# A decoder layer on one core: where cross-attention's inverse row sums are spread, and how many products the routing logits take

## The chip, the cores and the metric

One core of a Trainium2 chip runs one program. The metric is device time in microseconds, the median over runs. The engines are TensorE (PE; its weight loads, PEld, overlap the products), VectorE (DVE), ScalarE (ACT), GpSimd (POOL) and SyncE (SP), which issues the transfers.

## What is computed

A decoder layer on 16 sequences of 128 tokens, width 512, fp32: self-attention, cross-attention with a context, and a mixture of experts with routing. Only cross-attention and the routing logits are touched:

```python
probs = jax.nn.softmax(scores, axis=-1)            # 16 heads, clipped and masked scores
probs = probs / (probs.sum(axis=-1, keepdims=True) + 1e-08)
ctx = jnp.einsum('bhst,bhtd->bhsd', probs, v)      # heads of 32 columns
delta = ctx @ Wo.T + bo                            # then scaled, normed, added to x
...
logits = x @ gate_weight.T                         # x normed again, 64 experts
scores = jax.nn.softmax(logits, axis=-1)
```

## The kernel before

Three phases follow each other, each ended by a barrier: `self_phase`, `cross_phase` (324 to 647 us of the trace) and `feed_forward`. Every fp32 product that needs its precision is split in a high and a low half and done as three products (`matmul3`, L41 to L43: low by high, high by low, high by high).

`cross_phase` walks over the 16 sequences t, which this text calls steps; a step is taken to run from one `scores` to the next. The order on each engine is written out by hand in the loops over t, and semaphores tie the engines together. TensorE does in step t: `scores(t)` (L1967); `widen(t - 1)` (L1994); a projection ("unit") of 12 products for a later sequence; in even steps from 4 on `positions` (L2056 to L2061), which waits until the first half of step t's scores has been read, and from 6 on later `table_part` (L2082), which waits for the second half; a second unit; `turn_final(t - 2)` (transposes of the normed result); `project_out(t - 1)`; `logits(t - 2)`; a third unit; `sums(t)` (L1976) and `attend_v(t)` (L1987). Steps 0 to 11 have three units each; steps 12 and 13 have none, steps 14 and 15 two each, of the shared expert. In steps 3, 7 and 11 all units are queries, and the second needs the bank that ACT empties of the third unit of the step before only after `exps(t, 0)`.

The softmax is normed after the product with the values. `sums(t)` leaves the 16 row sums of a sequence in one bank: row 32 j + c holds head 4 c + j. VectorE inverts all 128 rows (`row_sums`, L1682). The `widen` of the next step multiplies the inverses by four 0/1 matrices (`spread`), which fills a bank with each inverse repeated over its head's 32 rows, ACT copies it to SBUF (`rinv_out`, L1470), and VectorE multiplies the attended values by it (`attn_out`, L1688).

VectorE does in step t: `delta(t - 2)` (L1709 to L1717); `bounded(t, 0)` (L1674, half of the scores); `attn_out(t - 1)`; `bounded(t, 1)`; `attn_lo(t - 1)` (from step 12 on on POOL); in even steps from 4 on `place_tokens` and `keep_slots` (L1793 to L1831); `x_lo` (L1667); in odd steps from 3 on `rank_experts` (L1735 to L1754); `final_lo(t - 2)` (L1722, from step 12 on on POOL), which frees TensorE's logits; statistics; `output(t - 1)` (L1701 to L1705) after the output projection; `route_max(t - 2)` (L1727), the greatest logit, read from PSUM; in odd steps from 3 on `choose_experts` (L1762 to L1783); `row_sums(t)`. ACT's `route_exp` (L1550) reads the logits from PSUM too and frees their bank. After step 15 the same pieces run out in a tail, in which VectorE ranks and places the last two groups of tokens and completes the table of the experts' tokens that the next phase starts from (L1910).

Of the kernel before, what the change touches and what calls it, by code (L numbers as in the profile page):

```python
# [6 lines left out]
F32R = mybir.dt.float32r  # L7
# [953 lines left out]
def cross_uses():  # L961
# [3 lines left out]
    for t in range(BATCH + 2):  # L965
        units = cross_units(t)
        proj += units[0:2]
        ex[1] += [("rb", t - 1)] if 1 <= t <= BATCH else []
# [13 lines left out]
def cross_phase(nc, x_in, ctx_in, pieces, vecs, out_x, stage, kept, early, route, ident, shared):  # L982

    with ExitStack() as ctx:
# [25 lines left out]
        gate = [sb("gate_hi", [P, KC, E], F32R), sb("gate_lo", [P, KC, E], F32R)]  # L1010
# [17 lines left out]
        spread = sb("spread", [P, KC, HPC, HD])  # L1028
# [51 lines left out]

        lneg = sb("lneg", [P, BATCH])
# [41 lines left out]
        s_sum, s_rinv, s_rb = sem("sums_in_psum"), sem("rinv_ready"), sem("rinv_in_psum")  # L1123
# [7 lines left out]
        s_lg, s_lm = sem("logits_in_psum"), sem("logit_max_ready")  # L1131
# [136 lines left out]
        def _(pool):  # L1268
# [66 lines left out]
            def constants():  # L1335
# [4 lines left out]
                lk(pool.memset(spread[:], 0.0))  # L1340
                lk(pool.affine_select(out=spread[:], in_=spread[:], pattern=[[-1, KC], [-HD, HPC], [0, HD]],
                                      compare_op=ALU.not_equal, fill=1.0, base=0, channel_multiplier=1))
# [62 lines left out]
        def _(act):  # L1405
# [60 lines left out]
            def rinv_out(t):  # L1466
                act.wait_ge(s_rb, t + 1)
                if t:
                    act.wait_ge(s_er[0], exchanged(0, ("pv", t - 1)))
                act.activation(rb[:], ex[1][:], ACT.Copy).then_inc(s_er[1], 1)  # L1470

# [73 lines left out]
            def route_exp(t):  # L1545
                g = group_of(t)
                act.wait_ge(s_lm, t + 1)
                if g >= 2:
                    act.wait_ge(s_choice, g - 1)
                act.activation(prob[g % 2][:, t - CROSS_GROUPS[g][0], :], ex[0][:, 0:E], ACT.Exp, bias=lneg[:, t:t + 1],  # L1550
                               accum_out=lsum[:, t:t + 1]).then_inc(s_er[0], 1)
# [7 lines left out]
            for t in range(BATCH):  # L1559
# [6 lines left out]
                if t >= 1:  # L1566
                    rinv_out(t - 1)
# [37 lines left out]
            rinv_out(BATCH - 1)  # L1605
# [22 lines left out]
        def _(dve):  # L1628
# [49 lines left out]
            def row_sums(t):  # L1678
                dve.wait_ge(s_sum, t + 1)
                if t:  # L1680
                    dve.wait_ge(s_rb, t)
                dve.reciprocal(rinv[:], ex[1][:, 0:P]).then_inc(s_er[1], 1)  # L1682

            def attn_out(t):
                dve.wait_ge(s_pv, t + 1)
                dve.wait_ge(s_er[1], exchanged(1, ("rb", t)))
# [38 lines left out]
            def route_max(t):  # L1725
                dve.wait_ge(s_lg, t + 1)
                dve.tensor_reduce(lneg[:, t:t + 1], ex[0][:, 0:E], AX, ALU.max, negate=True).then_inc(s_lm, 1)  # L1727

            def rank_experts(g):
# [4 lines left out]
                dve.wait_ge(s_er[0], exchanged(0, ("lg", b - 1)))  # L1734
# [109 lines left out]
            for t in range(BATCH):  # L1844
# [5 lines left out]
                if t >= 1:  # L1850
                    attn_out(t - 1)
# [36 lines left out]
            one, two, three = range(NG - 3, NG)  # L1888
            delta(BATCH - 2)
# [23 lines left out]
        def _(pe):  # L1913
# [77 lines left out]
            def widen(t):  # L1991
                out = exchange(1, ("rb", t))
                for c in range(KC):
                    ins = pe.matmul(out[:, c * P:(c + 1) * P], spread[:, c, :, :].rearrange("p j d -> p (j d)"), rinv[:],  # L1994
                                    start=True, stop=True)
                ins.then_inc(s_rb, 1)

# [12 lines left out]
            def logits(t):  # L2010
                out = exchange(0, ("lg", t))[:, 0:E]
# [5 lines left out]
                for k in range(KC):  # L2017
                    ins = matmul3(pe, out, (hi[:, k, :], lo[:, k, :]), (gate[0][:, k, :], gate[1][:, k, :]),
                                  k == 0, k == KC - 1)
                ins.then_inc(s_lg, 1)  # L2020

            def shared_unit(i):
# [6 lines left out]
                else:  # L2029
# [3 lines left out]
                    elif i == EARLY + 1:  # L2033
                        pe.wait_ge(s_er[1], exchanged(1, ("rb", BATCH - 1)))
# [51 lines left out]
            for t in range(BATCH):  # L2086
# [3 lines left out]
                if t >= 1:  # L2090
                    widen(t - 1)
# [37 lines left out]
            widen(BATCH - 1)  # L2129
# [1040 lines left out]
```

## Time and profile before

| | |
|---|---|
| three runs | 1549.15, 1557.19, 1557.39 us; median 1557.19 |
| profiled execution, first to last instruction | 1550.6 us |
| its busy time | PE 1471.4 (95%), DVE 1132.1 (73%), ACT 959.0 (62%), POOL 724.0 (47%) |
| cross-attention in it | from 324 to 647 us |

The profiled execution shows no time of its own beside its span, 1550.6 us, which lies between the fastest run and the median. Busy shares are averages over three very different phases; what matters is the stretch from 324 to 647 us and who waits there for whom.

### The profile page before, as it was taken

The numbers are of one execution on the slowest core, as the hardware profiler recorded it, in microseconds if no ns is written. First come the engines' busy times: TensorE is split into PE (matmuls) and PEld (weight loads), VectorE is DVE, ScalarE is ACT, GpSimd is POOL, SyncE is SP. The second block draws the span as 40 slices with busy tenths as digits, with TensorE's granted clock in tenths as the row PEclk, the third lists the DMA queues.
The fourth block names the chain that finished last, engine by engine and source line by source line (L and its number), as shares of the span: only waits on it lengthen the run. The fifth ranks groups of instructions, "written<-read, shape, count | busy, mean of one in ns | idle before, by whom it ended". The sixth has DMA issues, their size and how long they took to land.

```text
span 1550.6 us, 30285 instructions
## 1 busy us (share of the span) xinstructions
PE 1471.4 (95%) x10344; PEld 1217.4 (79%) x10344; DVE 1132.1 (73%) x2021; ACT 959.0 (62%) x1897; POOL 724.0 (47%) x894
## 2 busy tenths in 40 slices
PE   6999998999999979599999999999999999999898
PEld 4788887778888767488888888888888888776675
DVE  6677666745888788777777787777777787757666
ACT  4566566644566566677777777777777777731111
POOL 2122225242232155356565655556565655447573
PEclk9999999999999999899999999999999999999999
DMA  6012112332221231398787778777787778567574
GB/s 211 1 63 82 51 60 70 103 93 75 63 76 42 71 108 38 122 370 298 265 296 265 262 259 286 271 268 262 265 297 265 261 261 285 183 213 246 149 216 156
DMA packets 116629, 280.25 MB, mean 181 GB/s; under 512 B 17984, under 2 KB 23104, under 8 KB 116544
## 3 DMA queue, kind: packets, MB, share of 16 engines
q1 hardware_dynamic: 98800, 228.25, 43.4%
q0 software_dynamic: 15360, 50.34, 10.1%
q8 instruction: 52, 0.85, 0.2%
q10 hardware_dynamic: 2384, 0.53, 0.2%
q14 instruction: 33, 0.27, 0.1%
HBM read 235.69 MB, written 43.38 MB: 180 GB/s over the span
## 4 chain that ended last, share of the span: by engine, by line
PE 48%; DVE 3%; issue 2%; POOL 2%; DMA 1%; another core or an unknown queue 1%; ACT 0%; DVEq 0%; SPq 0%; POOLq 0%
PE e_gu L2608 19%; PE e_gu L2610 9%; PE e_dn_rest L2636 6%; PE e_tr L49 3%; PE e_dn_main L41 3%; PE e_dn_main L43 3%; PE e_dn_main L42 3%; DVE h_acc L2901 2%; POOL h_yk L2818 1%; DMA h_yk<-y_dram,h_idx 1%; DVE h_h_raw L2932 0%; DMA e_raw_u<-in_L_ffn_Wu_dram 0%; DVE h_hid L2917 0%; PE h_gt L41 0%
## 5 line engine op out<-in xcount | busy, mean ns | idle before, releaser
L2371 POOL TENSOR_TENSOR e_hid<-e_h_raw,e_hid 128x128 fp32r<-128x128 f32 (+1 forms) x192 | 165.6, 863 | 223.4 <-ACT e_hid L2436 223.4
L2608 PE MATMUL e_gu<-e_xT_hi_lo,e_wg 128*128 128x384 f32 (+1 forms) x768 | 231.9, 358 | 0.6 <-issue 0.6
L2608 PE MATMUL e_gu<-e_xT_hi_lo,e_wu 128*128 128x384 f32 (+1 forms) x768 | 230.6, 356 | 0.0
L2610 PE MATMUL e_gu<-e_xT_hi_lo,e_wu 128*128 128x192 f32 (+1 forms) x768 | 193.4, 252 | 0.0
L2610 PE MATMUL e_gu<-e_xT_hi_lo,e_wg 128*128 128x192 f32 (+1 forms) x768 | 193.2, 252 | 0.0
L2379 POOL TENSOR_TENSOR e_wd<-e_raw_d,e_wd 96x512 fp32r<-96x512 f32 x64 | 131.4, 2053 | 36.1 <-ACT e_wd L2421 36.1
L2431 ACT ACTIVATE e_low<-e_gu 128x384 f32<-128x384 f32 (+1 forms) x192 | 93.2, 486 | 83.5 <-PE e_gu L2610 56.2
L2514 DVE TENSOR_TENSOR e_total<-e_gu,e_low 128x384 f32<-128x384 f32 (+1 forms) x192 | 105.6, 550 | 53.3 <-issue 44.5
L2608 PEld LDWEIGHTS e_gu<-e_xT_hi_lo,e_wg 128*128 128x128 f32 (+1 forms) x768 | 138.3, 180 | 5.8 <-issue 1.6
L2610 PEld LDWEIGHTS e_gu<-e_xT_hi_lo,e_wg 128*128 128x128 f32 (+1 forms) x768 | 140.1, 182 | 1.4
L2608 PEld LDWEIGHTS e_gu<-e_xT_hi_lo,e_wu 128*128 128x128 f32 (+1 forms) x768 | 137.9, 180 | 3.8
L2610 PEld LDWEIGHTS e_gu<-e_xT_hi_lo,e_wu 128*128 128x128 f32 (+1 forms) x768 | 139.8, 182 | 0.0
L2503 DVE TENSOR_TENSOR e_wg<-e_raw_g,e_wg 128x1408 fp32r<-128x1408 f32 x64 | 104.0, 1625 | 45.6 <-ACT e_wg L2412 45.6
L2818 POOL DMA_INDIRECT h_yk<-y_dram,h_idx x96 | 103.3, 1076 | 28.7 <-issue 25.5
L2421 ACT ACTIVATE e_wd<-e_raw_d 128x1024 fp32r<-128x1024 f32 (+1 forms) x128 | 106.4, 831 | 0.0
L2520 DVE TENSOR_TENSOR e_h_raw<-e_total,e_h_raw 128x192 f32<-128x192 f32 (+1 forms) x192 | 84.7, 441 | 27.8 <-ACT e_h_raw L2426 27.8
L2503 DVE TENSOR_TENSOR e_wu<-e_raw_u,e_wu 128x1408 fp32r<-128x1408 f32 x64 | 103.9, 1623 | 1.1 <-ACT e_wu L2412 1.1
L2359 POOL DMA_INDIRECT e_xg<-xf_dram,e_idx x93 | 93.0, 1000 | 22.1 <-issue 16.7
L2412 ACT ACTIVATE e_wg<-e_raw_g 128x1408 fp32r<-128x1408 f32 x64 | 88.3, 1380 | 10.2 <-DMA e_raw_g<-in_L_ffn_Wg_dram 10.2
L505 ACT ACTIVATE s_prb<-s_prb,s_nmax 128x128 f32<-128x128 f32 x256 | 80.0, 393 | 23.2 <-DVE s_nmax L632 23.1
L2636 PE MATMUL e_dn_rest<-e_raw_d,e_h_raw 128*64 128x512 f32 (+1 forms) x384 | 89.5, 601 | 0.0
L2412 ACT ACTIVATE e_wu<-e_raw_u 128x1408 fp32r<-128x1408 f32 x64 | 88.0, 1375 | 1.0 <-DMA e_raw_u<-in_L_ffn_Wu_dram 1.0
(426 smaller groups left out, 3953.7 us busy)
## 6 DMA issues: line engine op xcount, KB each, us to landing
e_raw_g<-in_L_ffn_Wg_dram SPq DMA_DIRECT2D x64, 704.0 KB
e_raw_u<-in_L_ffn_Wu_dram SPq DMA_DIRECT2D x64, 704.0 KB
e_raw_d<-in_L_ffn_Wd_dram SPq DMA_DIRECT2D x64, 512.0 KB, 6.2
y_dram<-e_y_main SPq DMA_DIRECT2D x64, 256.0 KB
e_raw_d<-in_L_ffn_Wd_dram SPq DMA_DIRECT2D x64, 192.0 KB, 7.5
y_dram<-e_y_rest SPq DMA_DIRECT2D x64, 128.0 KB
s_xr<-in_x_dram SPq DMA_DIRECT2D x16, 256.0 KB, 4.1
x_dram<-s_x SPq DMA_DIRECT2D x16, 256.0 KB, 2.7
```

The lines of the kernel that those rows point to most:

```text
L2359: pool.indirect_dma_start(out=xg[:, j * H:(j + 1) * H], out_offset=None, in_=xf, in_offset=bass.IndirectOffsetOnAxis(ap=ids[:, j:j + 1], a ...
L2371: pool.tensor_tensor(hid[b][1][0:n, c, :], h_raw[g.odd][b][0:n, c, 0:P], hid[b][0][0:n, c, :].bitcast(F32), ALU.subtract).then_inc(s_hl, 1)
L2379: pool.tensor_tensor(wd[b][1][0:96, 2, :], raw_d[g.odd][b][0:96, 2, :], wd[b][0][0:96, 2, :].bitcast(F32), ALU.subtract).then_inc(s_dp[b], 1)
L2412: act.activation(w[b][0][:], raw[b][:], ACT.Copy).then_inc(s_guh[b], 1)
L2421: act.activation(wd[b][0][0:rows, cs, :], raw_d[g.odd][b][0:rows, cs, :], ACT.Copy).then_inc(s_dh[b], 1)
L2431: act.activation(low[m][0:n], gu[m][0:n, :, CAP:2 * CAP], ACT.Copy).then_inc(s_low, 1)
L2503: dve.tensor_tensor(w[b][1][:], raw[b][:], w[b][0][:].bitcast(F32), ALU.subtract).then_inc(s_gul[b], 1)
L2514: dve.tensor_tensor(total[0:n, c], gu[m][0:n, :, 0:CAP], low[m][0:n], ALU.add).then_inc(s_sum, 1)
L2608: pe.matmul(bank[0:n, 0:2 * CAP], w[b][0][:, k, m:m + n], xT[:, :, k, toks], start=k == 0, stop=False)
L2610: ins = pe.matmul(bank[0:n, 0:CAP], w[b][1][:, k, m:m + n], xT[:, 0, k, toks], start=False, stop=k == KC - 1)
L2636: ins = pe.matmul(dn_rest[b * REST:(b + 1) * REST, :], h_raw[g.odd][b][0:n, c, P:CAP], raw_d[g.odd][b][0:n, c, :], start=c == 0, stop=c == 2)
L2818: pool.indirect_dma_start(out=yk[b][:, k * H:(k + 1) * H], out_offset=None, in_=y_in, in_offset=bass.IndirectOffsetOnAxis(ap=idx[b][:, k:k ...
```

## The change

`widen`, `rinv_out` and the constant `spread` go. In their place VectorE does `spread_rinv(t - 1)`, four shuffles of 128 rows by 128 columns from `rinv` to `rb`, each within groups of 32 rows, between `bounded(t, 0)` and `attn_out(t - 1)`; in the tail right after the last `row_sums`, ahead of `delta(14)`. The two halves of the gate's weights lie side by side, so that the high half of x is multiplied by both in one product of 128 columns, and the low half by the gate's high half in one of 64: 8 products instead of 12. The logits then stand in two halves in PSUM; VectorE adds them into an SBUF tile (`tensor_reduce` over the pair), waits for that, and takes the maximum; `route_exp` reads the SBUF tile. The exchange bank of the logits is freed by the addition, not by ACT.

```diff
@@ -965,7 +965,6 @@
         proj += units[0:2]
-        ex[1] += [("rb", t - 1)] if 1 <= t <= BATCH else []
         ex[1] += [("x", m) for m in cross_fresh(t)]
@@ -1007,7 +1006,8 @@
         wo = [sb("wo_hi", [P, KC, H], F32R), sb("wo_lo", [P, KC, H], F32R)]
-        gate = [sb("gate_hi", [P, KC, E], F32R), sb("gate_lo", [P, KC, E], F32R)]
+        gate_both = sb("gate_hi_lo", [P, KC, 2, E], F32R)
+        gate = [gate_both[:, :, half, :] for half in range(2)]
         bias_q = kept["bias_q"]
@@ -1025,7 +1025,6 @@
         pick = sb("pick", [P, KC, HD])
-        spread = sb("spread", [P, KC, HPC, HD])
         iota8 = sb("iota8", [P, GROUPS])
@@ -1078,6 +1077,7 @@
 
+        logit = sb("logit", [P, E])
         lneg = sb("lneg", [P, BATCH])
@@ -1120,7 +1120,7 @@
         s_sc, s_exp, s_clip = sem("scores_in_psum"), sem("exp_ready"), sem("scores_bounded")
-        s_sum, s_rinv, s_rb = sem("sums_in_psum"), sem("rinv_ready"), sem("rinv_in_psum")
+        s_sum, s_rb = sem("sums_in_psum"), sem("rinv_spread")
         s_pv, s_ah, s_al = sem("pv_in_psum"), sem("attnT_hi_ready"), sem("attnT_lo_ready")
@@ -1128,7 +1128,8 @@
         s_ft, s_fh, s_fl = sem("xfT_in_psum"), sem("xfT_hi_ready"), sem("xfT_lo_ready")
-        s_lg, s_lm = sem("logits_in_psum"), sem("logit_max_ready")
+        s_lg, s_lm = sem("logit_halves_in_psum"), sem("logit_max_ready")
+        s_le = sem("logit_exp_ready")
         s_choice, s_pos, s_posr = sem("choice_ready"), sem("positions_in_psum"), sem("positions_read")
@@ -1337,9 +1338,6 @@
                 lk(pool.memset(pick[:, 0, KC:HD], 1.0))
-                lk(pool.memset(spread[:], 0.0))
-                lk(pool.affine_select(out=spread[:], in_=spread[:], pattern=[[-1, KC], [-HD, HPC], [0, HD]],
-                                      compare_op=ALU.not_equal, fill=1.0, base=0, channel_multiplier=1))
                 pool.memset(mark[:], 0.0).then_inc(s_pick, 1)
@@ -1463,12 +1461,6 @@
 
-            def rinv_out(t):
-                act.wait_ge(s_rb, t + 1)
-                if t:
-                    act.wait_ge(s_er[0], exchanged(0, ("pv", t - 1)))
-                act.activation(rb[:], ex[1][:], ACT.Copy).then_inc(s_er[1], 1)
-
             def attn_hi(t):
@@ -1547,8 +1539,8 @@
                     act.wait_ge(s_choice, g - 1)
-                act.activation(prob[g % 2][:, t - CROSS_GROUPS[g][0], :], ex[0][:, 0:E], ACT.Exp, bias=lneg[:, t:t + 1],
-                               accum_out=lsum[:, t:t + 1]).then_inc(s_er[0], 1)
+                act.activation(prob[g % 2][:, t - CROSS_GROUPS[g][0], :], logit[:], ACT.Exp, bias=lneg[:, t:t + 1],
+                               accum_out=lsum[:, t:t + 1]).then_inc(s_le, 1)
 
@@ -1563,8 +1555,6 @@
                         split_hi(n)
-                if t >= 1:
-                    rinv_out(t - 1)
                 exps(t, 0)
@@ -1602,7 +1592,6 @@
                     shared_hi(i)
-            rinv_out(BATCH - 1)
             shared_out(4)
@@ -1678,12 +1667,20 @@
                 if t:
-                    dve.wait_ge(s_rb, t)
+                    dve.wait_ge(s_rb, KC * t)
                 dve.reciprocal(rinv[:], ex[1][:, 0:P]).then_inc(s_er[1], 1)
+
+            def spread_rinv(t):
+
+                dve.wait_ge(s_er[1], exchanged(1, ("sum", t)))
+                if t:
+                    dve.wait_ge(s_er[0], exchanged(0, ("pv", t - 1)))
+                for c in range(KC):
+                    dve.stream_shuffle(rb[:, c * P:(c + 1) * P], rinv[:], [c] * HD).then_inc(s_rb, 1)
 
...
                 dve.wait_ge(s_pv, t + 1)
-                dve.wait_ge(s_er[1], exchanged(1, ("rb", t)))
+                dve.wait_ge(s_rb, KC * (t + 1))
                 dve.wait_ge(s_al, t + 1)
@@ -1724,14 +1721,19 @@
                 dve.wait_ge(s_lg, t + 1)
-                dve.tensor_reduce(lneg[:, t:t + 1], ex[0][:, 0:E], AX, ALU.max, negate=True).then_inc(s_lm, 1)
+                if t:
+                    dve.wait_ge(s_le, t)
+                dve.tensor_reduce(logit[:], ex[0][:, 0:2 * E].rearrange("p (h e) -> p e h", h=2), AX, ALU.add
+                                  ).then_inc(s_er[0], 1)
+                dve.wait_ge(s_er[0], exchanged(0, ("lg", t)))
+                dve.tensor_reduce(lneg[:, t:t + 1], logit[:], AX, ALU.max, negate=True).then_inc(s_lm, 1)
 
...
                 grouped = pr.rearrange("p t (g n) -> p (t g) n", g=GROUPS)
-                dve.wait_ge(s_er[0], exchanged(0, ("lg", b - 1)))
+                dve.wait_ge(s_le, b)
                 link(dve.reciprocal(lsum[:, a:b], lsum[:, a:b]))
@@ -1848,6 +1850,7 @@
                 if t >= 1:
+                    spread_rinv(t - 1)
                     attn_out(t - 1)
@@ -1886,6 +1889,7 @@
             one, two, three = range(NG - 3, NG)
+            spread_rinv(BATCH - 1)
             delta(BATCH - 2)
@@ -1988,13 +1992,6 @@
 
-            def widen(t):
-                out = exchange(1, ("rb", t))
-                for c in range(KC):
-                    ins = pe.matmul(out[:, c * P:(c + 1) * P], spread[:, c, :, :].rearrange("p j d -> p (j d)"), rinv[:],
-                                    start=True, stop=True)
-                ins.then_inc(s_rb, 1)
-
             def project_out(t):
@@ -2008,15 +2005,16 @@
             def logits(t):
-                out = exchange(0, ("lg", t))[:, 0:E]
+                out = exchange(0, ("lg", t))
                 if t < LAST - 2:
...
                 for k in range(KC):
-                    ins = matmul3(pe, out, (hi[:, k, :], lo[:, k, :]), (gate[0][:, k, :], gate[1][:, k, :]),
-                                  k == 0, k == KC - 1)
+                    pe.matmul(out[:, 0:2 * E], hi[:, k, :], gate_both[:, k, :, :].rearrange("p h e -> p (h e)"),
+                              start=k == 0, stop=False)
+                    ins = pe.matmul(out[:, 0:E], lo[:, k, :], gate[0][:, k, :], start=False, stop=k == KC - 1)
                 ins.then_inc(s_lg, 1)
@@ -2031,7 +2029,7 @@
                     elif i == EARLY + 1:
-                        pe.wait_ge(s_er[1], exchanged(1, ("rb", BATCH - 1)))
+                        pe.wait_ge(s_er[1], exchanged(1, ("sum", BATCH - 1)))
                     elif i == EARLY + 2:
@@ -2087,8 +2085,6 @@
                 scores(t)
-                if t >= 1:
-                    widen(t - 1)
                 for i in EARLY_UNITS.get(t, ())[0:1]:
@@ -2126,7 +2122,6 @@
             shared_unit(4)
-            widen(BATCH - 1)
             positions(BATCH, one)
```

## Rows read from the trace of the kernel before

**Rows 1.** Chain that ended last, by engine (the page's section 4).

```profile
PE 48%; DVE 3%; issue 2%; POOL 2%; DMA 1%; another core or an unknown queue 1%; ACT 0%; DVEq 0%; SPq 0%; POOLq 0%
```

**Rows 2.** Stretches of cross-attention: us, busy and count by engine, PEclk, DMA share, GB/s.

```profile
342.25:539.06 196.81, 195.11 (x1929) 161.76 (x1925) 151.05 (x418) 114.25 (x194) 49.56 (x97) 1.00 0.19 59
539.06:603.07 64.01, 53.66 (x615) 44.13 (x611) 54.74 (x146) 43.69 (x79) 36.77 (x43) 0.95 0.31 94
603.07:647.20 44.13, 34.02 (x195) 26.78 (x192) 38.45 (x124) 27.06 (x53) 16.13 (x19) 0.96 0.16 57
```

**Rows 3.** Timeline of PE, steps 8 and 9: start, length, engine, line.

```profile
478.27 0.19 PE L41 MATMUL c_ex<-c_gate_hi,c_xfT_lo 128*128 128x64 f32 x1
...
479.53 0.48 PE L41 MATMUL c_pj<-a_xT_hi,a_wqk_lo 128*128 128x512 f32 x1
...
485.44 1.16 PE L1994 MATMUL c_ex<-c_rinv,c_spread 128*128 128x128 f32 x8
...
486.35 0.47 PE L41 MATMUL c_pj<-a_xT_hi,a_wqk_lo 128*128 128x512 f32 x1
```

**Rows 4.** Forms of the tile c_gmax, c_posn and timeline: nearest VectorE instructions.

```profile
L1737 DVE TENSOR_REDUCE c_gmax<-c_prob x9: 220/286/286, 382.7 to 632.2; 128x16 f32<-128x128 f32 x7, 128x8 f32<-128x64 f32 x2
...
L1794 DVE TENSOR_TENSOR c_posn<-c_sc,c_count x9: 203/271/273, 399.6 to 640.3; 128x128 f32<-128x128 f32 x7, 128x64 f32<-128x64 f32 x2
...
472.58 1.02 DVE L1799 TENSOR_TENSOR a_stage<-a_stage,c_posn 128x384 f32<-128x384 f16 x2
```

**Rows 5.** Timeline of DVE and PE, steps 2, 6 and 8 to 10.

```profile
367.66 0.69 DVE L1722 TENSOR_TENSOR c_xfT_lo<-c_ex,c_xfT_hi 128x512 fp32r<-128x512 f32 x1 [1.57 <-ACT c_xfT_hi L1485]
...
440.09 0.67 DVE L1722 TENSOR_TENSOR c_xfT_lo<-c_ex,c_xfT_hi 128x512 fp32r<-128x512 f32 x1
...
441.50 0.19 PE L41 MATMUL c_ex<-c_gate_hi,c_xfT_lo 128*128 128x64 f32 x1
...
464.96 0.96 DVE L1682 RECIPROCAL c_rinv<-c_ex 128x128 f32<-128x128 f32 x1
...
476.35 0.69 DVE L1722 TENSOR_TENSOR c_xfT_lo<-c_ex,c_xfT_hi 128x512 fp32r<-128x512 f32 x1 [0.31 <-ACT c_xfT_hi L1485]
...
482.45 1.08 PE L1976 MATMUL c_ex<-c_prT,c_pick 128*32 128x128 f32 x32
...
483.60 0.96 DVE L1682 RECIPROCAL c_rinv<-c_ex 128x128 f32<-128x128 f32 x1 [3.05 <-PE c_ex L1976]
...
491.58 0.69 DVE L1667 TENSOR_TENSOR a_xT_lo<-c_ex,a_xT_hi 128x512 fp32r<-128x512 f32 x1 [1.07 <-ACT a_xT_hi L1426]
...
494.87 0.69 DVE L1722 TENSOR_TENSOR c_xfT_lo<-c_ex,c_xfT_hi 128x512 fp32r<-128x512 f32 x1
...
496.01 0.28 PE L41 MATMUL c_ex<-c_gate_hi,c_xfT_lo 128*128 128x64 f32 x1
...
500.29 1.08 PE L1976 MATMUL c_ex<-c_prT,c_pick 128*32 128x128 f32 x32
...
502.40 0.95 DVE L1682 RECIPROCAL c_rinv<-c_ex 128x128 f32<-128x128 f32 x1
```

**Rows 6.** Timeline of PE, step 11.

```profile
526.91 0.50 PE L41 MATMUL c_pj<-a_xT_hi,a_wv_lo 128*128 128x512 f32 x1 [0.53 <-ACT a_qkT L1458]
```

**Rows 7.** Timeline of PE, steps 12 and 13.

```profile
543.30 0.27 PE L2056 MATMUL c_sc<-c_diag_pos,c_chosen 128*64 128x128 bf16 x2 [1.98 <-DVE c_prT L1674]
...
544.98 2.10 PE L2082 MATMUL c_sc<-c_entry,a_stage 128*64 128x192 f16 x12 [1.14 <-issue]
...
561.13 0.47 PE L41 MATMUL c_pj<-c_wo_hi,c_aT_lo 128*128 128x512 f32 x1 [0.19 <-POOL c_aT_lo L1295]
```

**Rows 8.** Timeline of DVE and PE in the tail.

```profile
605.18 0.95 DVE L1682 RECIPROCAL c_rinv<-c_ex 128x128 f32<-128x128 f32 x1
...
611.56 0.47 PE L41 MATMUL c_pj<-c_wo_hi,c_aT_lo 128*128 128x512 f32 x1 [0.31 <-POOL c_aT_lo L1295]
...
645.75 0.18 DVE L1910 COPY table<-table 64x64 f32<-64x64 f32 x1
```

## The prediction

> **What bounds the kernel now.** I read the chain that ended last, then busy time by stretch, then the timelines of single steps. The chain begins in the expert phase and nothing of cross-attention is on it but through the barrier before that phase, so a microsecond gained before the barrier is one gained at the end [rows 1]. In steps 1 to 11 TensorE is busy 195.1 of 196.8 us at a granted clock of 1.00 (2.4 GHz) and VectorE 151.1; in steps 12 to 15 the order turns, VectorE 54.7 of 64.0 and TensorE 53.7, and in the tail VectorE has 38.5 of 44.1 [rows 2]. So TensorE bounds the first stretch and VectorE the other two, by this view. The timeline corrects it: `rank_experts` and `choose_experts` make VectorE late in odd steps. In step 9 the sums begin at 500.29 and their inverse could follow 1.15 us behind, as in step 8 (482.45 to 483.60), at 501.44; it starts at 502.40, because VectorE is still choosing [rows 5]. And TensorE's logits wait for `final_lo`, which stands late in VectorE's queue: it ends 0.45 us before the logits in step 9 (495.56, 496.01), 0.74 in step 6 (440.76, 441.50) and 1.23 in step 8 (477.04, 478.27) [rows 3, 5]. That is the slack which decides this change.
>
> **What is removed.** `widen` holds TensorE from 485.44 to 486.35, 0.91 us a step. Logits hold it from 478.27 to 479.53, 12 products in 1.26 us, 0.11 apiece beyond the first; four fewer save 0.44 us [rows 3]. ACT's copy, 0.60 us, goes from an engine with slack. On POOL two instructions of the start go; nothing waits there. A TensorE-bound step would be 1.35 us shorter, step 1, without logits, 0.91.
>
> **What is added, all on VectorE.** No row shows a shuffle. Nearest are 128 columns in a reduction, 0.29 us, or an addition from PSUM, 0.27. Two additions of 384 columns take 1.02 us together and 0.55 singly, so a follower without a wait hides 0.08 of its time [rows 4]. Four shuffles then take 4 x 0.29 - 3 x 0.08 = 0.92 us. Low bound: 0.5, if the columns pass at twice the rate of these rows. High bound: 2.2, if a shuffle of 128 columns costs the 0.55 of an addition of 384. I take 0.92, the value of the rows of its own size. They stand behind `bounded(t, 0)`, and behind them wait `attn_out`, `bounded(t, 1)`, `attn_lo`, placing or ranking, and `final_lo`; who waits for these is TensorE's `table_part`, `project_out` and logits, and ACT's second exponential. The logits' addition reads 128 columns of PSUM, 0.27 us, and the maximum waits for it, 0.04: 0.31 us a step (bounds 0.2 and 0.5), ahead of `choose_experts` and `row_sums`. The exchange bank of the logits is free some 0.3 us sooner; no step hangs on it.
>
> The Trainium skill, page "VectorE: DVE Perf Modes", section "The DRAIN you can't avoid", says that the next instruction doesn't start until the pipeline is empty. By that rule the shuffles take 1.16 us. The pair of 1.02 us contradicts it [rows 4].
>
> **Step by step.** I add up the distance between one inverse and the next.
> - Steps 1 to 4 are TensorE's. VectorE waits there for ACT, 1.57 us ahead of `final_lo` in step 2 [rows 5], which swallows the shuffles. Step 1 gains 0.9, step 2 1.35. In steps 3, 7 and 11 the second unit waits for a bank that ACT empties behind `exps(t, 0)`, already 0.53 us late in step 11 [rows 6]; that chain runs over VectorE and isn't shortened, so `widen`'s 0.91 is lost and 0.44 stays. Step 4 gains 1.2. Sum 3.9.
> - Step 8: `final_lo` ends 0.92 - 0.31 (its old wait) = 0.61 later, at 477.65; logits start at 477.7 and not 478.27, the sums 0.44 sooner yet: 1.0 gained, not 1.35. Step 6 has no such wait: 440.76 + 0.92 = 441.68, logits 0.2 later than now, less 0.44: 0.2 gained. Step 10 I take between them, 0.4 [rows 3, 5].
> - Steps 5 and 9: of the shuffles' 0.92 the wait of 1.07 for ACT swallows about half [rows 5], as ACT itself follows `attn_out`; `final_lo` comes 0.4 later, so the logits start when they do now, and VectorE, the bound to the next inverse, is 0.4 + 0.31 later: 0.7 lost each.
> - Step 7 gains 0.3, step 11, where VectorE is full to the end, loses 0.3. Steps 5 to 11 together gain 0.2.
> - Step 12: TensorE idles 1.98 us for `bounded(12, 0)`, then for `bounded(12, 1)` ahead of `table_part` [rows 7]. `widen` sits in the first idle time and buys nothing; the second wait grows by 0.92 and moves all that follows: 0.92 - 0.44 + 0.31 = 0.8 lost. Step 14 has the same pieces: 0.8. In step 13 `project_out` waits for `attn_lo` already [rows 7], 0.4 later by the shuffles with 0.31 for the addition: 0.7 lost. Step 15 gains 0.2. Sum -2.1.
> - Tail: the inverse at 605.18 is followed by the shuffles, and all behind it on VectorE up to 645.75 is late by 0.92; `project_out` already waits for that chain, by 0.31 [rows 8]. Two additions come on top: 1.5 lost.
>
> Sum: 3.9 + 0.2 - 2.1 - 1.5 = 0.5 us gained. The profiled execution, 1550.6 us, would become 1550.1; it lies 6.6 us under the median of 1557.19, and on the median the same 0.5 gives 1556.7. The three runs themselves span 8.2 us, more than anything in this sum. About 0.5%, 7.8 us, is what a measurement can tell from no change.
>
> **Rivals.**
> - *TensorE stays the bound.* If the shuffles fall into VectorE's waits everywhere up to step 11, the gain is 0.91 + 10 x 1.35 - 3 x 0.91 = 11.7 us: 1545.5. For it: the waits of 3.05 us for the sums [rows 5], VectorE busy 77% [rows 2]. Against: those waits lie behind `final_lo`, not before it. 15%.
> - *Every VectorE instruction stands alone.* 1.16 instead of 0.92, in the ten places where it isn't swallowed (steps 4 to 6, 8 to 10, 12 to 14, tail): 2.4 us more, 1559.1. This is the Trainium skill's rule of the same page and section. 12%.
> - *Dear shuffles, slower.* The price per shuffle decides: over 10 places the change is 7.8 us slower from 0.92 + 0.83 = 1.75 us for four, 0.44 each. At 2 us it is 10.8 - 0.5 slower: 1567.5. For it: no row shows one. Against: 0.44 is half again the 0.29 of its size [rows 4]. 8%.
> - *The clock.* TensorE idles more where its clock already dips: granted mean 0.95 in steps 12 to 15, and in step 12 twelve short products took 2.10 us, 0.175 apiece, against 0.11 for a logit's [rows 2, 3, 7]. Three more groups like this, 12 x 0.065 = 0.8 us each, and an output projection slowed as much, cost 3 us or so: 1560. 8%.
> - *The wide product isn't paced like the others.* If 128 columns take 0.22 and not 0.11, the 0.44 goes; it counts in the ten steps 2 to 11: 4.4 lost, 1561. 5%.
>
> **The numbers.** The forecast has 52%, its own range 1552 to 1562 (shuffles between 0.5 and 1.45 in ten places: -4.2 to +5.3 us). Faster: the first rival and 7 points of the forecast whose runs fall at the low end, 0.22. Slower: the dear shuffles and 3 points from clock and product, 0.11. The rest is the same, 0.67. The range of 8 in 10 runs from 1546 to 1563: half of the first rival and the dear shuffles are left out, and the high bound of the shuffles with them.
>
> **What would show it.** Four shuffles between `bounded(t, 0)` and `attn_out(t - 1)`, some 0.9 us; TensorE's next unit right behind `scores`, 0.9 us sooner; logits in 0.85 us. In steps 5 to 10 VectorE's late chain: logits waiting for `final_lo`, where now they wait for nothing. Between the inverses of steps 0 and 4 3.9 us less, of 4 and 11 about the same, of 11 and 15 some 2 more. The barrier within 1 us of where it is. I am wrong if VectorE keeps waiting 3 us for the sums in even steps while TensorE never waits for `final_lo` (then 1545), or if a shuffle takes 0.4 us or more.

## Result and profile after

The changed kernel is slower. Sixteen runs of each, side by side: 1560.22 us (1555.61 to 1572.96) against 1554.05 (1549.06 to 1557.39), ratio 1.0052 with an interval of 1.0036 to 1.0068, so 8.1 us of 1554 (5.6 to 10.6); the medians themselves lie 6.2 us apart. The forecast was 0.5 us gained. Beside two later kernels it came to 1.0044 (1.0027 to 1.006).

The page of the profiled execution after (its own time 1555.61), busy time and the chain that ended last:

```profile
PE 1460.2 (94%) x10152; PEld 1201.8 (77%) x10152; DVE 1151.6 (74%) x2165; ACT 950.4 (61%) x1881; POOL 724.8 (47%) x892
...
PE 52%; issue 3%; DVE 1%; DMA 1%; another core or an unknown queue 1%; POOL 0%; ACT 0%; SPq 0%; POOLq 0%; DVEq 0%
```

TensorE works 11 us less than before, VectorE 20 more. The chain is TensorE's as in [rows 1] and in the expert phase; what happens ahead of the barrier only shifts it.

The stretches of cross-attention after; columns as in [rows 2]. They are cut at the starts of inverses: first to twelfth (steps 1 to 11), to sixteenth (12 to 15), and to the table's last copy (tail):

```profile
345.18:540.82 195.64, 183.75 (x1840) 148.08 (x1836) 164.39 (x515) 107.96 (x185) 49.41 (x97) 1.00 0.19 60
540.82:613.27 72.45, 53.38 (x570) 42.78 (x562) 61.63 (x185) 42.12 (x76) 36.56 (x43) 0.86 0.27 81
613.27:656.14 42.87, 31.22 (x163) 24.65 (x163) 37.79 (x131) 26.75 (x52) 16.04 (x18) 0.86 0.16 59
```

Cut the same way, the kernel before has 197.18, 66.42 and 40.57 us. So the first stretch is 1.5 us shorter, the second 6.0 longer, the tail 2.3: 6.8 us more. And the granted clock, 0.95 and 0.97 before in the last two, is 0.86; a mean of 0.86 of 2.4 GHz makes a good quarter of them at the lower level, 1.2 GHz. In the first stretch it is 1.00 in both.

The timeline of VectorE after, a step's shuffles, a step's logits and the cast of step 6:

```profile
433.18 1.21 DVE L1663 TENSOR_SCALAR c_prT<-c_sc 128x1024 f32<-128x1024 f32 x1
...
434.31 0.29 DVE L1679 STREAM_SHUFFLE c_rb<-c_rinv 128x128 f32<-128x128 f32 x1
...
434.52 0.30 DVE L1679 STREAM_SHUFFLE c_rb<-c_rinv 128x128 f32<-128x128 f32 x1
...
434.93 0.30 DVE L1679 STREAM_SHUFFLE c_rb<-c_rinv 128x128 f32<-128x128 f32 x1
435.32 0.69 DVE L1685 TENSOR_TENSOR c_attn<-c_ex,c_rb 128x512 f32<-128x512 f32 x1
...
441.08 1.29 DVE L1832 CAST slot<-c_posm 128x12 uint32<-128x12 f32 x1
...
462.87 0.27 DVE L1726 TENSOR_REDUCE c_logit<-c_ex 128x64 f32<-128x128 f32 x1
463.18 0.22 DVE L1729 TENSOR_REDUCE c_lneg<-c_logit 128x1 f32<-128x64 f32 x1
```

A shuffle takes 0.29 to 0.30 us and the next starts 0.21 behind it; from the first to `attn_out` it is 1.01. The logits' addition keeps the maximum 0.31 behind. Both prices are the forecast's.

The timeline of TensorE after, at the places of [rows 7, 8]; the first row is of step 6, the next three of step 12, three of step 14, two of the tail:

```profile
443.77 0.30 PE L2015 MATMUL c_ex<-c_gate_hi_lo,c_xfT_hi 128*128 128x128 f32 x1 [1.55 <-DVE c_xfT_lo L1719]
...
545.35 0.39 PE L2054 MATMUL c_sc<-c_diag_pos,c_chosen 128*64 128x128 bf16 x2 [3.83 <-DVE c_prT L1663]
...
548.06 2.10 PE L2080 MATMUL c_sc<-c_entry,a_stage 128*64 128x192 f16 x12 [1.88 <-issue]
...
554.21 0.22 PE L2015 MATMUL c_ex<-c_gate_hi_lo,a_shared_x_hi 128*128 128x128 f32 x1
...
580.37 0.39 PE L2054 MATMUL c_sc<-c_diag_pos,c_chosen 128*64 128x128 bf16 x2 [3.46 <-DVE c_prT L1663]
...
583.08 2.10 PE L2080 MATMUL c_sc<-c_entry,a_stage 128*64 128x192 f16 x12 [1.88 <-issue]
...
588.44 0.60 PE L49 MATMUL c_ex<-ident,a_stage 128*128 128x128 f32 x4
...
619.71 1.11 PE L49 MATMUL c_ex<-ident,a_stage 128*128 128x128 f32 x4 [4.63 <-ACT a_stage L1436]
...
624.89 0.22 PE L2015 MATMUL c_ex<-c_gate_hi_lo,c_xfT_hi 128*128 128x128 f32 x1
```

TensorE idles 3.83 us ahead of step 12's `positions`, where it idled 1.98, and 1.88 ahead of `table_part` for 1.14 [rows 7]. Behind these gaps short products pass at about half pace: `table_part` of step 14 takes 2.10 us, where the kernel before took 1.15, in TensorE's timeline before:

```profile
577.52 1.15 PE L2082 MATMUL c_sc<-c_entry,a_stage 128*64 128x192 f16 x12 [0.79 <-issue]
```

### The profile page after: what moved, and what is told of

The parts are those of the page before. It is cut to its first block, busy times and chain, and to the rows that moved or that the text cites. A ratio compares the mean times of both kernels' runs of the same rounds, so it can differ in the third digit from the quotient of the medians.

```text
span 1553.9 us, 30041 instructions
## 1 busy us (share of the span) xinstructions
PE 1460.2 (94%) x10152; PEld 1201.8 (77%) x10152; DVE 1151.6 (74%) x2165; ACT 950.4 (61%) x1881; POOL 724.8 (47%) x892
## 4 chain that ended last, share of the span: by engine, by line
PE 52%; issue 3%; DVE 1%; DMA 1%; another core or an unknown queue 1%; POOL 0%; ACT 0%; SPq 0%; POOLq 0%; DVEq 0%
PE e_gu L2603 19%; PE e_gu L2605 9%; PE e_dn_rest L2631 6%; PE e_tr L49 3%; PE e_dn_main L41 3%; PE e_dn_main L43 3%; PE e_dn_main L42 3%; PE h_dn L41 1%; PE h_dn L42 1%; PE h_dn L43 1%; PE h_gt L41 1%; DVE h_acc L2896 1%; PE h_gt L42 1%; PE h_gt L43 1%
```

## Experiments

All are read with one account: the distance between the starts of consecutive inverses, step by step, and from the last to the table's last copy. It is compared with the kernel before's profile (304.2 us in all). One profile of each kernel stands behind it; how far that bears is the first run's question. The table gives each kernel's difference, in us; "fc" is the forecast. The edits are excerpts, with "..." where lines are left out: e4, e5 and e8 against the changed kernel, the others against the kernel before.

| steps | fc | after | e2 | e3 | e4 | e5 | e6 | e7 | e8 | e9 | e10 |
|---|---|---|---|---|---|---|---|---|---|---|---|
| 1 to 4 | -3.9 | -3.5 | -2.2 | -1.2 | -3.6 | -2.6 | 0.0 | 0.0 | -3.5 | -3.5 | -3.5 |
| 5, 9 | 1.4 | 1.6 | 1.0 | 0.6 | 1.6 | 0.0 | 1.1 | 0.0 | 1.6 | 0.0 | 0.0 |
| 6 | -0.2 | 1.0 | 3.1 | -0.4 | 1.0 | -0.3 | 3.1 | 0.0 | -0.1 | -0.4 | -0.4 |
| 7, 11 | 0.0 | 1.0 | 0.0 | 0.7 | 1.0 | 0.0 | 0.0 | 0.0 | 1.0 | 0.0 | 0.0 |
| 8, 10 | -1.4 | -1.6 | -0.8 | -1.2 | -1.7 | -1.0 | 0.0 | 0.0 | -1.7 | -1.7 | -1.6 |
| 12 | 0.8 | 1.2 | 1.9 | 0.6 | -0.6 | 0.5 | 1.8 | -1.4 | -0.6 | 0.8 | -1.4 |
| 13 | 0.7 | 1.2 | 1.1 | 1.1 | 1.2 | 0.7 | 1.0 | -0.9 | 0.0 | 0.8 | -0.9 |
| 14 | 0.8 | 2.3 | 2.8 | 0.4 | 0.9 | 2.2 | 2.6 | 1.5 | 0.9 | 0.8 | 0.0 |
| 15 | -0.2 | 1.3 | -0.2 | 0.0 | 0.1 | -0.6 | 1.1 | 0.0 | 1.2 | 0.0 | 0.0 |
| tail | 1.5 | 2.3 | 2.8 | 1.2 | 1.2 | 0.7 | 1.8 | 0.0 | 2.8 | 1.3 | 0.0 |
| all | -0.5 | 6.8 | 9.4 | 1.7 | 1.1 | -0.4 | 12.4 | -0.9 | 1.6 | -1.9 | -7.9 |

**e1, the kernel before again**, unchanged.

> The kernel before, unchanged, for a second profile. Metric of all profiles: the distance from the first inverse of the row sums (step 0) to the table's last copy, 304.2 us in the first profile and 311.0 in the changed kernel. If these are properties of the kernels, this one gives 304.2 within 0.5; if such distances wander by several us from one execution to the next, no account by steps can stand. The span may wander by some us outside cross-attention.

Measured: 1550.76 us. Every step as in the first profile within 0.05 us but step 13, 0.5 longer, at a granted clock of 0.82 and not 0.91; distance 304.7. The account can be trusted to half a microsecond and in steps 1 to 11 to a tenth. What lies behind it wanders by more (904.8 and 899.0 us from the table's last copy to the end of these two) and is not explained here.

**e2, the shuffles alone**, in place of `widen`; the logits keep their twelve products.

```diff
-                    ins = pe.matmul(out[:, c * P:(c + 1) * P], spread[:, c, :, :].rearrange("p j d -> p (j d)"), rinv[:],
-                                    start=True, stop=True)
...
+                for c in range(KC):
+                    dve.stream_shuffle(rb[:, c * P:(c + 1) * P], rinv[:], [c] * HD).then_inc(s_rb, 1)
```

> Only the shuffles, logits as before (12 products, maximum from PSUM). Theory V (the shuffles stand in VectorE's queue where TensorE waits for it, and the idle time that follows lowers TensorE's clock): all of the loss is here, distance 304.2 + 8 = 312, ratio 1.0055. Rival L (the logits' addition and its wait do it): distance at most 304.2, ratio 1.000 or less.

Measured: 1555.96 us against 1548.0, ratio 1.0062 (1.0047 to 1.0078), 9.4 us more distance. The whole loss comes with this half. Step 6, +3.1, shows how. The timeline of TensorE and then the windows of this kernel:

```profile
440.70 0.27 PE L41 MATMUL c_ex<-c_gate_hi,c_xfT_lo 128*128 128x64 f32 x1 [1.54 <-DVE c_xfT_lo L1716]
...
443.09 0.63 PE L41 MATMUL c_pj<-a_xT_hi,a_wv_lo 128*128 128x512 f32 x1
```

```profile
442.00:444.00 2.00, 2.00 (x8) 1.55 (x8) 0.46 (x4) 0.41 (x2) 0.74 (x2) 0.62 0.00 0
444.00:446.00 2.00, 2.00 (x7) 1.57 (x5) 0.00 (x0) 0.00 (x0) 0.00 (x0) 0.53 0.00 0
```

TensorE waits 1.54 us for `final_lo`; then the second unit's twelve products, 0.23 us apart in the kernel before, come 0.43 apart for 3 us, at a granted clock of 0.62 and 0.53. From 442.03 to 446.55 the unit takes 4.52 us, against 2.92 before: 1.6 lost behind 1.5 of waiting. The wait alone doesn't decide it: in the changed kernel the logits of step 6 wait 1.55 us (first row of TensorE's timeline after), and the unit behind them takes 2.93 at full pace.

**e3, the eight products alone**, the sum written into the tile of the probabilities.

```diff
+                dve.tensor_reduce(pr, ex[0][:, 0:2 * E].rearrange("p (h e) -> p e h", h=2), AX, ALU.add
+                                  ).then_inc(s_er[0], 1)
...
-                    ins = matmul3(pe, out, (hi[:, k, :], lo[:, k, :]), (gate[0][:, k, :], gate[1][:, k, :]),
+                    pe.matmul(out[:, 0:2 * E], hi[:, k, :], gate_both[:, k, :, :].rearrange("p h e -> p (h e)"),
+                              start=k == 0, stop=False)
+                    ins = pe.matmul(out[:, 0:E], lo[:, k, :], gate[0][:, k, :], start=False, stop=k == KC - 1)
```

> Only the logits' part: 8 products, halves added by VectorE, here written straight into the tile of probabilities; inverses spread by matrix products as before. Theory V: TensorE-bound steps 2 to 4, 6 to 8 and 10 shorten by 0.44 each, steps 5, 9, 11, 15 and the tail lengthen by 0.3 to 0.6: distance 302.6, ratio 0.999. Rival L: distance 308 or more, ratio 1.003 or more.

Measured: 1547.06 us against the same 1548.0, ratio 0.9999 (0.9989 to 1.001). Steps 2, 3, 4, 6 and 10 gain 0.40 to 0.44, step 8 0.8, steps 5, 7, 9 and 11 lose 0.3 to 0.35. In time this half is even. The distance missed its forecast: 305.8 and not 302.6, because steps 12 to 15 and the tail lost 3.3, with the granted clock at 0.88 and 0.91 there. Nor do the halves add: 9.4 and 1.7 apart, 6.8 together.

**e4, the changed kernel with idle products** in TensorE's gaps (128 x 512, into banks that are overwritten next): 20 in step 12, 20 in 13, 18 in 14, 20 in the tail.

```diff
+            def filler(use, n):
+                out = fill(use)
+                for k in range(n):
+                    pe.matmul(out, wo[0][:, k % KC, 0:P], wo[0][:, k % KC, :], start=True, stop=True)
```

> The changed kernel, with idle products on TensorE (128 by 128 by 512, results overwritten) where it waits in steps 12 to 14 and in the tail: 14 and 6 in step 12, 20 in step 13, 12 and 6 in step 14, 20 in the tail. Theory C (part of the loss is the lowered clock of these stretches): the granted clock stays at 1.0 there, groups that took 1.4 to 2 times as long go back to full speed, distance 311.0 - 4.5 = 306.5, ratio 1.002. Rival (clock dips beside the path): clock up, distance 311 or more as the filler delays real work.

Measured: 1545.47 us against the same 1548.0, ratio 0.9987 (0.9974 to 1.0001). More work on TensorE takes the loss of time away, though the distance stays 1.1 above the kernel before. Its windows and its timeline of TensorE, at the places of the rows after:

```profile
539.17:607.19 68.02, 61.58 (x628) 48.41 (x620) 62.70 (x185) 42.03 (x75) 36.56 (x43) 1.00 0.29 87
607.19:648.94 41.75, 34.61 (x183) 27.29 (x183) 37.66 (x131) 26.88 (x52) 16.08 (x18) 0.96 0.17 60
```

```profile
546.40 1.15 PE L2085 MATMUL c_sc<-c_entry,a_stage 128*64 128x192 f16 x12 [0.70 <-issue]
...
550.78 0.30 PE L2015 MATMUL c_ex<-c_gate_hi_lo,a_shared_x_hi 128*128 128x128 f32 x1
...
579.58 1.15 PE L2085 MATMUL c_sc<-c_entry,a_stage 128*64 128x192 f16 x12 [0.71 <-issue]
...
583.53 0.60 PE L49 MATMUL c_ex<-ident,a_stage 128*128 128x128 f32 x4
```

In step 12 it is 4.38 us from `table_part` to the first logit product, against 6.15 after: 1.77 of the step's 1.83 us difference. In step 14, from `table_part` to the transposes, 3.95 against 5.36: 1.41 of 1.40. So in these two steps the difference is TensorE's own pace and next to nothing else. Against the changed kernel, steps 12 to 15 and the tail are 5.6 us shorter. But step 15's part, 1.2, is not pace: the clock is 1.00 there in both kernels. It is a pair of small VectorE instructions, which take 0.28 us together elsewhere. Step 15 of the changed kernel and then of this one:

```profile
603.53 2.42 DVE L1750 TENSOR_TENSOR c_gone<-c_iota,c_gidf 128x24 f32<-128x24 f32 x2
```

```profile
598.63 1.29 DVE L1750 TENSOR_TENSOR c_gone<-c_iota,c_gidf 128x24 f32<-128x24 f32 x2
```

VectorE is busy 18.34 of 19.19 us in that step after and 17.17 of 18.01 here. e8 comes back to this pair. In the kernel before it takes 2.44 in step 15 in one profile and 1.3 in the other (e1), and the step is 17.9 us long in both: VectorE was busy 15.8 of them and had room. The change filled that room, so the same meeting now costs its full length.

**e5, no spreading at all.** The tile of spread inverses is a constant, so the norming is left out; neither products nor shuffles, nor ACT's copy. The logits are done as before.

```diff
-                for c in range(KC):
-                    dve.stream_shuffle(rb[:, c * P:(c + 1) * P], rinv[:], [c] * HD).then_inc(s_rb, 1)
...
+            link(dve.memset(rb[:], 0.01))
```

> The kernel before with neither the spreading products nor the shuffles: the tile of spread inverses is set once to a constant, so the outputs are not attention's, and all else runs as before. It takes TensorE's part of the change without VectorE's price. Sum by queues alone (the prediction's reading): steps 1 to 4, 8 and 10 shorter by some 0.6 to 1.2 each as in the shuffles-only run, steps 5, 7, 9 and 11 within 0.2 of before, and steps 12 to 15 and the tail no longer than before, since VectorE does nothing more: distance from the first inverse to the table's last copy about 299 to 300 (before 304.2), time about 1546 against 1550, ratio 0.997. Theory of the clock: steps 12 to 15 and the tail get longer although VectorE lost nothing, as TensorE idles 0.9 us more in each: some 2 us together, granted clock below before's 0.95 between 540 and 605 us, ratio 0.998 to 1.000.

Measured: ratio 0.9989 (0.9965 to 1.0013), distance 0.4 shorter where the queues alone gave 4 to 5. Windows of steps 12 to 15, and TensorE in step 14:

```profile
538.23:607.48 69.25, 56.15 (x604) 45.79 (x593) 56.82 (x150) 41.44 (x75) 36.68 (x43) 0.85 0.30 88
```

```profile
576.56 0.39 PE L2039 MATMUL c_sc<-c_diag_pos,c_chosen 128*64 128x128 bf16 x2 [2.77 <-DVE c_prT L1660]
...
578.24 2.10 PE L2065 MATMUL c_sc<-c_entry,a_stage 128*64 128x192 f16 x12 [0.86 <-issue]
```

VectorE does nothing more than before (56.8 us busy in steps 12 to 15, 57.1 before), and still steps 12 to 15 and the tail lose 3.5 us: the clock is 0.85, `table_part` 2.10. Here less work on TensorE went with a slower TensorE. Whether the missing work or the shift of these steps in time did it, this run can't tell, since steps 1 to 11 are 3.9 us shorter too; e9 bears on that.

**e6, the shuffles added and the products kept**, into the tile that `attn_out` overwrites.

```diff
+                for c in range(KC):
+                    dve.stream_shuffle(attn[:, c * P:(c + 1) * P], rinv[:], [c] * HD).then_inc(s_rinv, 1)
```

> The kernel before with four shuffles more in each step, at the place that the change gives them, into a tile that the next instruction overwrites; the spreading products stay. It takes VectorE's price without TensorE's gain, and TensorE is busier by 0.9 us a step than in the shuffles-only run. Sum by queues alone: 0.9 to 1.0 us more where VectorE sets the pace (steps 5, 9, 12 to 15, the tail: some 7 us), 0 to 0.5 in steps 1 to 4, 6 to 8, 10 and 11, distance about 312, ratio 1.005. Theory of the clock: steps 12 to 15 and the tail gain less than the 8.3 us that the shuffles-only run showed there, some 4 to 5, because the products stay and TensorE idles less; granted clock between 540 and 605 us between 0.84 and 0.95. If they gain 8 us or more here too, the spreading products do not matter for the clock. Cast beside GpSimd's subtraction: step 6 may again lose 1.1 us where they meet.

Measured: ratio 1.0058 (1.0037 to 1.0079). Steps 5 and 9 lose 0.55 each, step 6 3.1 as in e2. Here I missed: steps 12 to 15 and the tail lose 8.2 us, as much as in e2, with the products in place. The window of steps 12 to 15 and step 12 of TensorE:

```profile
547.33:620.19 72.86, 59.14 (x636) 48.88 (x625) 60.56 (x182) 44.35 (x79) 36.57 (x43) 0.88 0.27 84
```

```profile
554.61 2.10 PE L2092 MATMUL c_sc<-c_entry,a_stage 128*64 128x192 f16 x12 [2.21 <-issue]
```

TensorE idles 2.21 us for late VectorE, 1.14 before [rows 7], though it has no less to do, and the clock is lower all the same. By the measure set beforehand (8 us or more here too) the spreading products do not matter for the clock. Of the two ways to make TensorE idle, 3.5 us and 8.2 apart come to 8.3 together (e2): they don't add. Step 14 alone orders itself by the products: its granted clock is 0.81 to 0.82 in the four profiles without `widen` (after, e2, e5, e11), 0.90 to 0.91 in e3, e6 and e9, which keep it, and 1.00 in both of the kernel before.

**e7, the kernel before with idle products**: 12, 14, 12 and 6, eight of step 14's ahead of `widen`.

```diff
+                if t == 14:
+                    filler(("f", 0), 8)
                 if t >= 1:
                     widen(t - 1)
+                if t == 12:
+                    filler(("o", t - 1), 8)
+                if t == 13:
+                    filler(("o", t - 1), 14)
...
+                        if t in (12, 14):
+                            filler(("o", t - 1) if t == 12 else ("f", 1), 4 if t == 12 else 4)
...
+            filler(("o", BATCH - 1), 6)
```

> The kernel before with idle 128x512 products in TensorE's gaps of steps 12 to 14 and the tail (12, 14, 12 and 6 of them), writing into banks whose content is overwritten. Theory of the clock: the kernel before loses little to it (0.95 of full speed between 540 and 605 us, 0.5 to 1 us of the distance), so the distance falls from 304.2 to 303 to 304 and the ratio is 0.999 to 1.0; against this kernel the changed one with fillers (305.3) is still slower by 1.5 to 2 us. Rival, the fillers do something else than keep the clock (they would then give about 5 us here as they did in the changed kernel): distance below 300.

Measured: ratio 0.9988 (0.9968 to 1.0007). Steps 12 and 13 gain 1.4 and 0.9, step 14 loses 1.5: its fillers stand ahead of `widen`, where TensorE, early by now, hardly idled. The kernel before lost to the clock as well: 2.3 us in steps 12 and 13, where I had written 0.5 to 1 in all.

**e8, e4 with GpSimd's subtraction of step 6 held** until VectorE's `x_lo`.

```diff
+                    if t == 6 and m == cross_context(t)[0]:
+                        pool.wait_ge(s_er[1], exchanged(1, ("x", cross_fresh(t)[0])))
                     context_lo(m)
```

> The changed kernel with fillers, and in step 6 GpSimd's two 1.26 us subtractions of the context's low part wait until VectorE has done its own subtraction of that step, which stands behind the cast of the slots. Theory of the shared port: the cast takes 0.17 us again and not 1.30, step 6 goes from +1.0 to about -0.1 against before, every other step within 0.3 of the fillers' run, distance about 304.2 (305.3 without), ratio 0.998. Rival, the step is lengthened by something else (the longer step 5 ahead of it, the logits' wait for the low part): step 6 stays at +0.7 to +1.0 with the cast at 0.17.

Measured: ratio 1.0009 (0.9989 to 1.0028). First GpSimd's timeline of the changed kernel, then VectorE's and GpSimd's of this one:

```profile
441.05 2.52 POOL L1286 TENSOR_TENSOR a_xT_lo<-a_qkT,a_xT_hi 128x512 fp32r<-128x512 f32 x2 [5.28 <-ACT a_xT_hi L1416]
```

```profile
439.40 0.17 DVE L1834 CAST slot<-c_posm 128x12 uint32<-128x12 f32 x1
```

```profile
440.31 2.53 POOL L1286 TENSOR_TENSOR a_xT_lo<-a_qkT,a_xT_hi 128x512 fp32r<-128x512 f32 x2 [6.24 <-DVE a_xT_lo L1658]
```

After, the cast began 0.03 us behind GpSimd's first subtraction, of 1.26 us, and lasted until that ended, 1.29. Held apart it takes 0.17, and step 6 goes from +1.0 to -0.1, the forecast's -0.2. The Trainium skill, page "SBUF — State Buffer", section "SBUF: two separate sides", has a rule for this: a VectorE instruction with two SBUF inputs or in a mode that uses both ports, and a GpSimd instruction, lock the port pair that they share for a whole instruction, and the later one stands still. The trace agrees in the standing still; whether the cast, with one input, runs in such a mode no run shows.

But the total didn't follow: the distance is 305.8 and not 304.2. Step 13 is 1.2 us shorter than in e4, step 15 and the tail 2.7 longer. Steps 13 and 15 are meetings of the same kind, moved by the earlier start. In e4 the pair `c_gone` takes 2.42 us in step 13 and 1.29 in step 15; here it takes 2.41 in step 15 and 1.3 in step 13, and the two steps follow. GpSimd's and VectorE's timelines of this pair, in step 13 of e4:

```profile
561.15 1.34 POOL L1321 TENSOR_TENSOR a_shared_gate_lo<-a_shared_raw,a_shared_gate_hi 128x512 fp32r<-128x512 f32 x1
...
562.45 1.29 POOL L1321 TENSOR_TENSOR a_shared_up_lo<-a_shared_raw,a_shared_up_hi 128x512 fp32r<-128x512 f32 x1
```

```profile
562.59 2.42 DVE L1750 TENSOR_TENSOR c_gone<-c_iota,c_gidf 128x24 f32<-128x24 f32 x2
```

The tail's 1.6 is another matter. The window of this kernel at the end of step 15 and the start of the tail:

```profile
600.00:610.00 10.00, 8.91 (x89) 6.70 (x82) 9.54 (x34) 1.81 (x4) 1.97 (x3) 0.66 0.01 2
```

The granted clock is 0.66, where e4 had 1.00 from 598 to 608 us; why it falls is open. A microsecond saved early moved the later steps against each other.

**e9, both kernels in one.** Shuffles for row sums 0, 1, 3, 7 and 9, eight products in steps 2, 3, 4, 6, 8 and 10, the old code elsewhere, and GpSimd held in step 6.

```diff
+SHUFFLED = (0, 1, 3, 7, 9)
+EIGHT = (0, 1, 2, 4, 6, 8)
...
-                if t >= 1:
+                if t >= 1 and t - 1 not in SHUFFLED:
                     widen(t - 1)
```

> Both kernels in one: shuffles only for the steps whose spreading they shorten (row sums 0, 1, 3, 7 and 9, spread in steps 1, 2, 4, 8 and 10), eight products only for the logits issued in steps 2, 3, 4, 6, 8 and 10, spreading products and twelve products elsewhere, and GpSimd's subtraction of step 6 behind VectorE's. Theory of the account by steps: the steps that TensorE paces keep the gains of the earlier runs (-0.9, -1.1, -0.4, -1.2, -0.4, -1.0, -0.6 in steps 1, 2, 3, 4, 6, 8, 10), steps 5, 7, 9 and 11 are as before, and steps 12 to 15 and the tail within 1 us of before, since TensorE's work there is the old one: distance 298 to 300 against 304.2, ratio 0.997. Rival, the gain is only moved: the later steps, VectorE's or a wait for a transfer, take 3 us or more of it back, and the distance is above 302.

Measured: 1543.0 us, ratio 0.997 (0.9957 to 0.9983), faster than both. Steps 1 to 11 gain 5.6 us, as the account said. Then steps 12 to 15 and the tail, whose code is that of before, lose 3.7, at granted clocks of 0.88 and 0.91. Here I missed: the distance is 302.3, not 298 to 300, and the rival (3 us or more taken back, above 302) came true. Step 12 of TensorE:

```profile
541.83 0.39 PE L2101 MATMUL c_sc<-c_diag_pos,c_chosen 128*64 128x128 bf16 x2 [1.98 <-DVE c_prT L1689]
```

The same instruction behind the same gap of 1.98 us took 0.27 before [rows 7] and 0.39 here. The gap alone doesn't say whether the clock falls, and steps that nobody touched can lose to it when they come earlier.

**e10, the mixed kernel with idle products**: 12, 14, 4 and 6.

```diff
+                if t == 14:
+                    filler(("f", 0), 2)
...
+                if t == 12:
+                    filler(("o", t - 1), 8)
+                if t == 13:
+                    filler(("o", t - 1), 14)
...
+                        if t in (12, 14):
+                            filler(("o", t - 1) if t == 12 else ("f", 1), 4 if t == 12 else 2)
...
+            filler(("o", BATCH - 1), 6)
```

> The mixed kernel with idle products in TensorE's gaps of steps 12 to 14 and the tail (12, 14, 4 and 6 of them). Theory of the clock: granted clock 0.98 or more between 535 and 600 us, distance lower than the mixed kernel's by 1 to 2 us (297 to 298), ratio 0.995 to 0.997: faster than both kernels. Rival: the clock was no loss in the kernel before, so the fillers give nothing or cost up to 1 us.

Measured: 1535.86 us against 1547.03, ratio 0.9929 (0.9911 to 0.9948): the fastest of all. Its windows, steps 1 to 11 and 12 to 15:

```profile
343.86:535.49 191.63, 189.30 (x1884) 154.68 (x1880) 157.08 (x463) 111.57 (x191) 49.74 (x97) 1.00 0.18 61
535.49:599.57 64.08, 60.12 (x665) 48.51 (x654) 57.48 (x149) 43.80 (x79) 36.76 (x43) 1.00 0.32 96
```

The clock is 1.00 and the distance 7.9 us below before, 6.0 below the same kernel without fillers, where 1 to 2 were expected. The ratio says 11 (8 to 14); what lies beyond the 7.9 is outside the account.

**e11, the changed kernel again.**

> The changed kernel again, beside the two mixed ones. Distance 311.0 within 0.6 as the first time, of which steps 1 to 11 within 0.1 of the first profile; ratio 1.005.

Measured: ratio 1.0044 (1.0027 to 1.006), distance 311.05 against 310.96, every step within 0.08. Its clock dips fall in the same places: in this kernel they belong to its timing, not to chance.

## Why the prediction was wrong

The instruction prices held. Four shuffles: 0.92 forecast, 1.01 measured, the rest because `attn_out` can't overlap the last one. The Trainium skill's page "VectorE: DVE Perf Modes", section "The DRAIN you can't avoid", lets the next instruction start only once the pipeline is empty, but excepts one that is not held back until all earlier ones have finished; the prediction took the rule without its exception. The rule would set the shuffles 0.30 apart; the trace has 0.21, which is the exception's case. Addition 0.31 and 0.31; eight products in 0.88 us, 0.11 apiece. The rivals of dear shuffles, of VectorE's lone instructions and of the wide product fell with these rows; that TensorE stays the bound fell in steps 5, 9 and 12.

- **Steps 1 to 4, 5 and 9, 8 and 10** came as forecast: -3.9, +1.4, -1.4 against -3.5, +1.6, -1.6. Steps 7 and 11 lost 1.0 and not 0: step 11's +0.3 was 0.7, and step 7's gain of 0.3 did not come; in e3 and after it loses 0.3, the size of the addition, so VectorE seems to pace it.
- **Step 6**, -0.2 against +1.0: I shifted `final_lo` by VectorE's delay and did not look what GpSimd does at the new time. The later cast met its subtraction; e8 shows it. Such meetings are in both kernels, and the change moves them. The pair `c_gone` of step 13, of the kernel before and then after, is shorter after:

```profile
561.11 2.40 DVE L1748 TENSOR_TENSOR c_gone<-c_iota,c_gidf 128x24 f32<-128x24 f32 x2
```

```profile
566.06 1.25 DVE L1750 TENSOR_TENSOR c_gone<-c_iota,c_gidf 128x24 f32<-128x24 f32 x2
```

- **Steps 12 to 15 and the tail** are the step that failed: 3.6 us forecast, 8.3 measured. The sum moved queues and left every instruction's duration as it was, TensorE's pace and VectorE's meetings with GpSimd alike. The queues themselves were nearly right. Against e10, whose code is the old one there and whose clock is held too, steps 12 and 14 of e4 are 0.8 and 0.9 longer, step 13 of e8 is 0.9, step 15 of e4 is 0.2 and its tail 1.2: 3.9 for a forecast of 3.6 (e4's own step 13 has 2.1, with the pair of 2.42 us in it). The pair in step 15 of the changed kernel adds 1.2, now that VectorE is full there. What remains is TensorE's pace. Fillers give back 1.8, 1.2, 1.4 and 1.1 us in steps 12, 13 and 14 and the tail of the changed kernel (step 13 against e8, where VectorE is as busy as after, 17.1 us), and 2.3 in the old code (before against e10), so the changed kernel loses 3.2 more. Queues 3.9, pace 3.2, the meeting 1.2 and steps 1 to 11 -1.5 make the 6.8. The pace is shown row by row for steps 12 and 14 and argued for 13 and the tail; the sum mixes profiles of several kernels and is good to some tenths.
- **The rival of the clock** had the mechanism that was missing, at 8%, with 3 us on top, and its price was met: 3.2. It belonged in the sum: step 12 already ran `table_part` at 2.10 [rows 7]. That its 1560 is where the median came to lie is half luck: the kernel before lay at 1554 beside it, and steps 6 and 15 lost 1.2 each by meetings that no rival had priced. Its reason, that TensorE idles more, is not shown. Less work and longer waits go with a lower clock in e5 and e6, but in e9 the untouched late code lost 6.0 to the pace (against e10), where the same code in the kernel before lost 2.3. So the point in time at which these steps begin matters as much, and how much of the 3.2 each of the three makes is open.

Open: how a gap must lie for the clock to fall (e9's row against [rows 7], e2's step 6 against the row after), why e8's tail slowed, and the 3 us or so by which ratios and distances differ.

## What to carry to other kernels

Before moving work off TensorE, look where its granted clock is below 1.00 or it idles behind another engine: there, less work, longer waits or merely another start can be paid in pace, and a few idle products in the gap may be worth more than the change (here 1.0052 became 0.9987, and in the mixed kernel 0.997 became 0.9929). A change made in every step of a pipeline is better made only in the steps whose bound it relieves; the account by steps tells which. Where an engine is shifted in time, see which instructions of VectorE and GpSimd meet at the new place.

## What the runs showed of the hardware

- A wait of 1.54 us was followed by 3 us of TensorE at 0.53 to 0.62 of its clock (e2), a wait of 1.55 us at the same place by none (after); a gap of 1.98 us was followed by a fast group in one kernel and a slow one in another (0.27 and 0.39 us).
- The granted clock of steps 12 to 15, 0.95 before (0.92 in e1), was 0.85 without the spreading products and ScalarE's copy (e5), and 0.88 in e9, where the code of these steps is unchanged; idle products raised it from 0.86 to 1.00 (e4) and from 0.88 to 1.00 (e10).
- A VectorE cast of 128x12 elements took 1.29 us instead of 0.17 beside a GpSimd subtraction that had begun 0.03 us earlier; a pair of VectorE instructions on 128x24 elements took 2.42 us instead of 0.28 beside two in a row.
- VectorE's shuffle of 128x128 fp32: 0.29 to 0.31 us, the next 0.21 us behind it, its mask load 11 to 17 ns.
